# Ternary chunks on GpSimd, a reordered start, and matmuls of 256 columns in a windowed attention kernel

## What is computed

```python
xn = _layernorm(x)                       # over 1024 features
q, k, v = xn @ w_q + b_q, xn @ w_k + b_k, xn @ w_v + b_v
# per head: softmax(q . k[-3..+3] / 8) over the 7 neighbours, times v
attn_out = out @ w_o + b_o
scale = max(mean(|weight|), 1e-5)
w_ternary = clip(round(weight / scale), -1, 1)
return x + attn_out + xn @ (w_ternary * scale).T
```

## Time and profile before

| | us |
|---|---|
| three runs | 678.44, 679.12, 680.46 |
| median | 679.12 |
| the profiled execution | 678.97 |
| its span on the slowest core (core 2) | 677.1 |
| TensorE busy | 629.9 (93%) |
| VectorE busy | 434.5 (64%) |
| ScalarE busy | 374.4 (55%) |
| GpSimd busy | 88.1 (13%) |

### The profile page before, as it was taken

One profiled execution on the slowest core, in us unless ns is written; L12 is line 12 of the kernel. 1 busy time (PEld: TensorE's weight loads), 2 busy tenths in 40 slices (PEclk: granted clock), 3 DMA queues, 4 the chain that ended last, 5 costly groups with the idle time before them and its releaser, 6 DMA issues.

```text
span 677.1 us, 11621 instructions; the slowest of 8 cores (671.6 to 677.1 us)
## 1 busy us (share of the span) xinstructions
PE 629.9 (93%) x3827; PEld 296.8 (44%) x3890; DVE 434.5 (64%) x534; ACT 374.4 (55%) x1418; POOL 88.1 (13%) x52
## 2 busy tenths in 40 slices
PE   1889986999999999999999999999899999999997
PEld 1344433444444444444444444444344444455543
DVE  6335888777666666666756676666666755566663
ACT  3453665555565545556555655555556555566573
POOL 1203000421111110111111111001011111111110
PEclk9989987999999999999999999999799999999999
DMA  8999997686554655556542665564453433334523
GB/s 192 206 207 283 154 154 164 161 204 140 126 139 127 156 141 139 124 114 131 134 103 84 146 136 141 140 154 112 89 114 86 100 82 94 92 97 106 146 78 93
DMA packets 129946, 91.17 MB, mean 135 GB/s; under 512 B 107872, under 2 KB 116192, under 8 KB 129888
## 3 DMA queue, kind: packets, MB, share of 16 engines
q1 hardware_dynamic: 121440, 82.05, 48.4%
q0 software_dynamic: 8448, 8.39, 8.9%
HBM read 55.82 MB, written 16.78 MB: 107 GB/s over the span
## 4 chain that ended last, share of the span: by engine, by line
PE 85%; DMA 5%; issue 3%; DVE 3%; ACT 3%; POOL 0%; DVEq 0%; ACTq 0%; SPq 0%; POOLq 0%
PE p_p L310 17%; PE p_p L335 16%; PE p_p L292 15%; PE p_f L460 15%; PE p_f L476 14%; PE p_s L363 3%; PE p_a L423 3%; DMA wq_b<-wq 3%; ACT sm L393 2%; DMA et<-en 1%; DVE sm L378 1%; DMA x<-x 1%; DVE en L406 1%; PE p_s L460 1%; PE p_p L553 1%
## 5 line engine op out<-in xcount | busy, mean ns | idle before, releaser
L393 ACT ACTIVATE sm<-sm,nmx 122x128 f32<-122x128 f32 x544 | 210.6, 392 | 15.7 <-DVE nmx L385 15.7
L489 POOL TENSOR_TENSOR xr<-xr,brow 128x1024 f32<-128x1024 f32 x32 | 75.4, 2360 | 507.7 <-DMA xr<-x 452.5
L292 PE MATMUL p_p<-xnt,wq_b 128*128 128x488 bf16 (+1 forms) x576 | 126.2, 367 | 4.0 <-ACT xnt L270 3.7
L310 PE MATMUL p_p<-xnt,wk_b 128*128 128x494 bf16 (+1 forms) x576 | 123.1, 360 | 0.0
L335 PE MATMUL p_p<-wv_b,xnt 128*128 128x512 bf16 x513 | 117.4, 381 | 4.9 <-issue 4.8
L300 ACT ACTIVATE qt<-p_p,bq 128x488 bf16<-128x488 f32 (+1 forms) x72 | 46.1, 640 | 135.6 <-PE p_p L292 135.5
L460 PE MATMUL p_f<-wft_b,xnt 128*128 128x512 bf16 x494 | 114.1, 385 | 0.5 <-DVE xr L494 0.4
L476 PE MATMUL p_f<-wo_b,att 128*128 128x512 bf16 x468 | 107.0, 379 | 5.5 <-issue 4.3
L378 DVE TENSOR_TENSOR sm<-p_s,mk_sb 122x1024 f32<-122x1024 f32 x68 | 82.9, 1219 | 34.1 <-PE p_s L363 34.1
L393 ACT ACTIVATION_READ_ACCUMULATOR sm<-sm,nmx 122x1 f32 x544 | 104.4, 192 | 0.0
L348 ACT CAST v<-p_p 128x512 bf16<-128x512 f32 x68 | 39.0, 576 | 103.1 <-PE p_p L335 103.1
(11 more groups left out here) (62 smaller groups left out, 277.4 us busy)
## 6 DMA issues: line engine op xcount, KB each, us to landing
xr<-x SPq DMA_DIRECT2D x32, 512.0 KB, 5.5
x<-x SPq DMA_DIRECT2D x31, 512.0 KB, 5.5
out<-xr SPq DMA_DIRECT2D x31, 512.0 KB, 3.4
wq_b<-wq POOLq DMA_DIRECT2D x4, 512.0 KB, 13.9
wk_b<-wk POOLq DMA_DIRECT2D x4, 512.0 KB, 15.5
xr<-wft SPq DMA_DIRECT2D x4, 512.0 KB, 11.4
wv_b<-wv POOLq DMA_DIRECT2D x4, 512.0 KB, 15.9
wo_b<-wo POOLq DMA_DIRECT2D x4, 512.0 KB, 25.7
```

The costliest lines, as they stand in the source:

```text
L292: q.do("tensor", lambda e, k=k: e.matmul(bank[:, 0:m], w_b["wq"][:, k * H + 128 * c:k * H + 128 * c + 128], rows_of(b, k, BQ * b + 3, m), ...
L310: q.do("tensor", lambda e, k=k: e.matmul(bank[:, 0:m], w_b["wk"][:, k * H + 128 * c:k * H + 128 * c + 128], rows_of(b, k, BQ * b, m), star ...
L393: q.do("scalar", lambda e, h=h: e.activation(sm[hf][0:TQ, KW * h:KW * h + KW], sm[hf][0:TQ, KW * h:KW * h + KW], AF.Exp, bias=nmx[hf][0:TQ ...
L489: q.do("gpsimd", lambda e: e.tensor_tensor(xr[t % NR][:, :], xr[t % NR][:, :], brow[:, :], ALU.add), ("xrb", t))
```

## The change

Four things change.

1. `v_job` and `f_proj` issue two matmuls of 256 columns for each of 512, each with its own weight load.
2. Ternary chunks 1, 2 and 3 are made by GpSimd (`terns_gpsimd`): two `tensor_scalar` and one subtraction each, with `bvb` as scratch. The other five (`terns_vector((6, 7, 4, 5, 0))`) are made by VectorE in a row, as before with two instructions each.
3. The copy that fills `bvb` moves from VectorE, early, to GpSimd, after chunk 3 (`value_bias`).
4. The order of the start: `wf_sum` apart from `wf_scale` and earlier; key job (1, 0) ahead of `scores(0, 0)`; all chunks ahead of `stats(8)`; `weights(0, 0)` and key job (1, 4) ahead of `scores(0, 1)`; the exponentials (0, 1) after both key jobs; the DMAs of `bo` and of the first three `xr` tiles at the end of the start instead of in step 0; the bias row in step 0 instead of step 1.

```diff
--- before.py
+++ after.py
@@ -192,7 +192,11 @@
         def bias_forms():
             q.need("vector", "bias")
             q.do("vector", lambda e: e.tensor_scalar_mul(bq8[:, :], bias[:, 0:8], 0.125), "bq8")
-            q.do("vector", lambda e: e.tensor_copy(
+
+        def value_bias():
+
+            q.need("gpsimd", "bias", ("ternk", 3))
+            q.do("gpsimd", lambda e: e.tensor_copy(
                 bvb[:, :].rearrange("p (c n) -> p c n", c=8, n=128),
                 bias[:, 16:24][:, :, None].broadcast_to([128, 8, 128])), "bvb")
 
@@ -332,10 +336,13 @@
             n, bank = next_bank()
             q.need("tensor", *weight("wv", jh), *[("xnt", b, r) for r in tiles_of(b)])
             for k in range(8):
-                q.do("tensor", lambda e, k=k: e.matmul(
-                    bank, rows_of(b, k, TQ * i, KW),
-                    w_b["wv"][:, k * H + 512 * jh:k * H + 512 * jh + 512],
-                    start=(k == 0), stop=(k == 7)), ("pj", n) if k == 7 else None)
+                for jq in range(2):
+                    lo = k * H + 512 * jh + 256 * jq
+                    q.do("tensor", lambda e, k=k, jq=jq, lo=lo: e.matmul(
+                        bank[:, 256 * jq:256 * jq + 256], rows_of(b, k, TQ * i, KW),
+                        w_b["wv"][:, lo:lo + 256],
+                        start=(k == 0 and jq == 0), stop=(k == 7 and jq == 1)),
+                        ("pj", n) if (k == 7 and jq == 1) else None)
             if jh == 1:
                 q.point[("v", i)] = q.point[("pj", n)]
             v_open[(i, jh)] = (n, bank)
@@ -450,17 +457,18 @@
         def f_proj(t):
             b = out_block(t)
             acc = p_out(t)
-            q.need("tensor", "wft", *[("xnt", b, r) for r in (t, t + 1)])
+            q.need("tensor", ("ternk", 0), ("ternk", 3), *[("xnt", b, r) for r in (t, t + 1)])
             if t == NO - 1:
                 q.need("tensor", ("sadd", NW - 1, 1))
             elif t >= 1:
                 q.need("tensor", ("out", t - 1))
             for k in range(8):
-                for jh in range(2):
-                    q.do("tensor", lambda e, k=k, jh=jh: e.matmul(
-                        acc[:, 512 * jh:512 * jh + 512], rows_of(b, k, KW * t + 3, KW),
-                        w_b["wft"][:, k * H + 512 * jh:k * H + 512 * jh + 512],
-                        start=(k == 0), stop=False), ("f", t) if (k == 7 and jh == 1) else None)
+                for jq in range(4):
+                    q.do("tensor", lambda e, k=k, jq=jq: e.matmul(
+                        acc[:, 256 * jq:256 * jq + 256], rows_of(b, k, KW * t + 3, KW),
+                        w_b["wft"][:, k * H + 256 * jq:k * H + 256 * jq + 256],
+                        start=(k == 0 and jq % 2 == 0), stop=False),
+                        ("f", t) if (k == 7 and jq == 3) else None)
 
         def o_proj(t):
             i = out_step(t)
@@ -516,10 +524,12 @@
                     w_b["wft"][:, k * H:(k + 1) * H], wf32[k], AF.Abs, accum_out=wab[:, k:k + 1]),
                     ("wabs", k))
 
-        def wf_scale():
+        def wf_sum():
             q.need("vector", *[("wabs", k) for k in range(8)])
             q.do("vector", lambda e: e.tensor_reduce(
                 wab[:, 8:9], wab[:, 0:8], AX.X, ALU.add), "wsum")
+
+        def wf_scale():
             q.need("tensor", "wsum", t_last[7])
             q.do("tensor", lambda e: e.matmul(
                 p_f[:, 0:1], ones[:, :], wab[:, 8:9], start=True, stop=True), "wtot")
@@ -533,18 +543,36 @@
             q.do("vector", lambda e: e.tensor_scalar_mul(wab[:, 10:11], wab[:, 9:10], 0.5))
             q.do("vector", lambda e: e.tensor_scalar_mul(wab[:, 11:12], wab[:, 9:10], -0.5), "wthr")
 
-        def wf_tern(j, k):
-            up = w_b["wft"][:, k * H:(k + 1) * H]
-            dn = brow[:, 512 * (j % 2):512 * (j % 2) + 512].bitcast(BF16)
+        def wf_tern(k, after, scratch):
+
             q.need("vector", "wthr")
-            if j >= 2:
-                q.need("vector", ("tern", j - 2))
+            if after is not None:
+                q.need("vector", after)
             q.do("vector", lambda e: e.tensor_scalar(
-                dn, wf32[k], wab[:, 10:11], None, ALU.is_gt), ("wup", k))
+                scratch, wf32[k], wab[:, 10:11], None, ALU.is_gt), ("wup", k))
             q.need("vector", ("wup", k))
             q.do("vector", lambda e: e.scalar_tensor_tensor(
-                up, wf32[k], wab[:, 11:12], dn, ALU.is_lt, ALU.subtract), ("tern", j))
-            q.point["wft"] = q.point[("ternk", k)] = q.point[("tern", j)]
+                w_b["wft"][:, k * H:(k + 1) * H], wf32[k], wab[:, 11:12], scratch,
+                ALU.is_lt, ALU.subtract), ("ternk", k))
+
+        def terns_vector(ks):
+            for n, k in enumerate(ks):
+                wf_tern(k, ("ternk", ks[n - 2]) if n >= 2 else None,
+                        brow[:, 512 * (n % 2):512 * (n % 2) + 512].bitcast(BF16))
+
+        def terns_gpsimd(ks):
+            q.need("gpsimd", "wthr")
+            for n, k in enumerate(ks):
+                up, dn = w_b["wft"][:, k * H:(k + 1) * H], bvb[:, :]
+                if n >= 1:
+                    q.need("gpsimd", ("ternk", ks[n - 1]))
+                q.do("gpsimd", lambda e, k=k, dn=dn: e.tensor_scalar(
+                    dn, wf32[k], wab[:, 10:11], None, ALU.is_gt), ("wup", k))
+                q.do("gpsimd", lambda e, k=k, up=up: e.tensor_scalar(
+                    up, wf32[k], wab[:, 11:12], None, ALU.is_lt), ("wdn", k))
+                q.need("gpsimd", ("wup", k), ("wdn", k))
+                q.do("gpsimd", lambda e, up=up, dn=dn: e.tensor_tensor(
+                    up, up, dn, ALU.subtract), ("ternk", k))
 
         def bias_half(jh):
             n, bank = next_bank()
@@ -559,10 +587,6 @@
                 brow[:, 512 * jh:512 * jh + 512], bank, brow[:, 512 * jh:512 * jh + 512],
                 ALU.add), ("pev", n))
             q.point["brow"] = q.point[("pev", n)]
-
-        def bias_row():
-            bias_half(0)
-            bias_half(1)
 
 
         x_load(0)
@@ -620,32 +644,28 @@
             wf_abs(k, "vector")
         for c in range(4):
             k_job(0, c, "scalar")
+        wf_sum()
+        k_job(1, 0, "scalar")
         scores(0, 0)
         mask_max(0, 0)
-        for c in range(3):
+        k_job(1, 1, "scalar")
+        wf_scale()
+        terns_gpsimd((1, 2, 3))
+        value_bias()
+        terns_vector((6, 7, 4, 5, 0))
+        stats(8)
+        for c in range(2, 4):
             k_job(1, c, "scalar")
-        wf_scale()
-        terns = list(enumerate((6, 7, 4, 5, 0, 1, 2, 3)))
-
-        def some_terns(lo, hi):
-            for j, k in terns[lo:hi]:
-                wf_tern(j, k)
-
-        some_terns(0, 2)
-        stats(8)
-        some_terns(2, 4)
-        k_job(1, 3, "scalar")
         for c in range(4, 8):
             exps(0, 0, range(2 * c - 8, 2 * c - 6))
             k_job(0, c, "scalar")
         rstd(8)
+        weights(0, 0)
+        k_job(1, 4, "scalar")
         scores(0, 1)
         mask_max(0, 1)
-        weights(0, 0)
-        some_terns(4, 6)
-        for c in range(4, 6):
-            k_job(1, c, "scalar")
-            exps(0, 1, range(4 * c - 16, 4 * c - 12))
+        k_job(1, 5, "scalar")
+        exps(0, 1)
         weights(0, 1)
         v_job(0, 0)
         v_evict(0, 0)
@@ -654,6 +674,11 @@
         k_job(1, 6, "scalar")
         e_transpose(0, 0)
         e_transpose(0, 1)
+
+        q.need("sync", ("ternk", 0))
+        q.dma("sync", "bo", lambda e: e.dma_start(brow[:, :], bo_h[:, :]), "bo")
+        for k in range(3):
+            xr_load(k)
 
 
         def stats_of_step(s):
@@ -725,8 +750,6 @@
                 e_transpose(n, 0)
             if t is not None:
                 f_proj(t)
-            if s == 0:
-                some_terns(6, 8)
             if n < NW:
                 exps(n, 1, range(4))
             att_v(s, 1)
@@ -739,12 +762,9 @@
                 weights(n, 1)
                 e_transpose(n, 1)
             if s == 0:
-                q.need("sync", "wft")
-                q.dma("sync", "bo", lambda e: e.dma_start(brow[:, :], bo_h[:, :]), "bo")
-                for k in range(3):
-                    xr_load(k)
+                bias_half(0)
+                bias_half(1)
             if t == 0:
-                bias_row()
                 xr_bias(0)
             if t is not None:
                 o_proj(t)
```

## The result

The changed kernel takes 683.32 us (median, 682.20 to 685.36) against 679.43 for the kernel before beside it: 1.0059 times as long, 95% interval 1.0040 to 1.0078, 4 us slower. The profiled execution took 683.32 us; its slowest core is core 6 with a span of 681.8 us.

What follows compares the result with a forecast made beforehand. The prediction took TensorE as the bound, except at the start, where it waits for VectorE. To 678.97 us it added 5.8 for a later step 2 and 3.1 for the 256-column matmuls: 687.9, forecast 688.0 us, range 676 to 693.

Runs made afterwards that it cites:

- b2: The changed kernel with 512-column matmuls again and the statistics of tile 8 ahead of VectorE's chunks; ratio 1.0068 to the kernel before.
- b1: The changed kernel with 512-column matmuls again and the first three `xr` loads at the end of step 0; ratio 1.0026 to the kernel before.

## What to carry to other kernels

Work given to GpSimd beside a busy VectorE is not free: what counts is for how long its instructions hold the ports and what VectorE has queued in that time, and a probe of tiny VectorE operations shows it. Before moving work ahead of a chain, count what stands ahead of the chain, not the largest wait in the list; the wait moves, the chain stays (b2). A DMA moved forward on SyncE is paid for by the transposes behind it on that queue, although the mean DMA share in that stretch (92.8 to 105.8 us) is only 0.61. What VectorE hands to SyncE late delays that queue too, even where VectorE itself has slack. And when rows of the same kind are merged, their length can hold a wait: the window has to be narrowed before it is read as a duration.

## What the runs showed of the hardware

GpSimd's `tensor_scalar` (1,024 columns, float32 to bfloat16, scalar from SBUF) takes 2.85 us alone, its bfloat16 subtraction of as many columns 2.12 us, the float32 addition 2.36 us: here fewer inputs are not cheaper. It holds the ports that it shares with VectorE for 0.9 us at its start and 0.7 us or more towards its end, and not between.

A matmul more for the same columns in all costs 2.0 to 2.3 ns with its own weight load at the 2.4 GHz level (37.32 against 37.45 us for two steps).

A DMA transpose's issue takes 1.2 us when nothing stands ahead of it, 1.24 us with only the 0.5 MB of `bo` issued before it (b1), and held SyncE for 4.1 and 5.5 us with 2 MB queued ahead. The changed kernel, core 6, from the chain that ended last and from the timeline:

```profile
98.99 4.14 SPq L257
...
103.21 5.54 SPq L257
...
116.90 1.23 SPq L257 DMA_TRANSPOSE xnt<-xn  x1
```
